# A two-layer graph network with residual norms: attention in float32 blocks, once a group, beside layer 0

## The chip, the cores and the metric

The kernel runs on one core of a Trainium2 chip. The metric is the device time of one execution in microseconds: 678.2 as the median of 3 runs (678.11 to 678.23). The core has five engines that run side by side, each with its own queue: TensorE (PE, its weight loads as PEld), VectorE (DVE), ScalarE (ACT), GpSimd (POOL) and SyncE (SP), which here issues the DMAs.

## What is computed

x is (128, 64, 512) in float32: 128 graphs of 64 nodes with 512 features. adj is 64 x 64 and shared. `reference`, cut to what matters:

```python
x = layernorm(x + einsum('bnf,nm->bmf', x, adj * adj) + bias)            # layer 0; its result is h
z_l, z_g, v = h @ W_lang.T, h @ W_grav.T, h @ W_V.T
A_l = relu(cos(z_l, z_l)) * not_eye                                       # 64 x 64 a graph
A_g = exp(-dist2(z_g, z_g) / (2 sigma^2)) * not_eye
K = w_l * rownorm(A_l * adj) + (1 - w_l) * rownorm(A_g * adj)
out = layernorm(h + (K @ v) @ W_O.T)                                      # layer 1
```

## The kernel before

It works on 16 groups (g) of 8 graphs. A group is held as 4 tiles (p) of 128 rows x 512, each tile two graphs of 64 nodes. The weights are folded once in a setup: T_L = W_lang'W_lang and T_G likewise (as the blocks of a triangle), and M = W_V'W_O'. So a group needs 12 projections (`project`, L360): 4 blocks each of y_L = T_L h and y_G = T_G h, and 4 tiles of u = h M. The float32 values are written as a sum of two float32r numbers, hi and lo, and a product is three float32r matmuls (hi·hi, hi·lo, lo·hi, from `parts`). So a projection of 128 x 512 has 3, 6, 9 or 12 matmuls of 512 columns: 108 in a group. They go through a ring of three PSUM banks: ACT rounds a bank to hi (`hi_proj`), DVE subtracts hi from it to get lo (`lo_proj`), and then the bank is free.

Attention takes a half group (q) at a time, two pairs of graphs. `gram` (L380) multiplies h by y for a pair (128 rows), both similarities in one matmul of 256 columns, 24 matmuls a half; since a pair's 128 x 128 result covers both graphs, its off-diagonal 64 x 64 blocks mean nothing and are zeroed by the mask `adj_bd`. ACT copies the result to P (`copy_p`), DVE takes its diagonal (`diagonals`) and subtracts it (shift), POOL makes inverse norms (`columns`), PE transposes P and the norms (`transpose_p`, L393 and L400), DVE adds, weighs and normalises (`similarities`, `coefficients`, `combine`), PE transposes K (`transpose_k`, L411), ACT and DVE split it, and `apply_k` (L424) multiplies K' by u with 3 matmuls of 512 columns for each p. POOL also makes the scale and the bias of both layernorms from DVE's counts; ACT applies them.

`layer0` (L320) is different: it is plain float32, and its 4 matmuls are blocks of 64 x 64 that lie in the four quarters of the array (`tile_position`), reading two 64-row halves of x and writing two halves of two banks:

```python
last = pe.matmul((bank_x, bank_p)[a][cols, :], mix[rows, rows], x_sb[g % 2][rows, 2 * h + c, :],
                 start=True, stop=True, tile_position=(a * N, c * N))
```

The order of work is written by hand, for each engine in a function `step(g)`: the projections of g, between them the second half of the attention of g - 1, layer 0 and the transposes of h of g + 1, and the gram of g. Semaphores hold the engines together. The last group and the end have an order of their own. DVE, ACT and POOL run their steps in a loop (`Fori`); PE's program is written out.

Of the kernel before, what the change touches and what calls it, by code (L numbers as in the profile page):

```python
# [5 lines left out]
def bass_two_layer_graph_resnorm(  # L19
# [13 lines left out]
    fp32r = mybir.dt.float32r  # L33
    ALU = mybir.AluOpType
    ACT = mybir.ActivationFunctionType

    B, N, D = x.shape
    R = 128
# [10 lines left out]
    PROJ = [(L, 3), (L, 0), (L, 2), (L, 1), (G, 3), (G, 0), (G, 2), (G, 1)] + [("u", p) for p in range(NP)]  # L49
# [4 lines left out]
    assert NG % 2 == 0 and NPROJ % NRING == 0  # L54

    def ring_of(k):

        return (NSETUP + k) % NRING

# [5 lines left out]
    with ctx:  # L65
# [8 lines left out]


        ident = sb("ident", [R, R])
        off_diag = sb("off_diag", [R, R])
        adj_bd = sb("adj_bd", [R, R])
        mask = sb("mask", [R, R])
        mix = sb("mix", [R, R])  # L80
# [5 lines left out]
        mixw = sb("mixw", [R, 4])  # L86
        pow_neg_half = sb("pow_neg_half", [R, 2])
# [7 lines left out]
        h_sb = [sb(f"h_sb{i}", [R, NP, D]) for i in range(2)]  # L95
# [9 lines left out]
        P_sb = [sb(f"P_sb{q}", [R, 2, 2, R]) for q in range(2)]  # L105
        diag_scr = sb("diag_scr", [R, 4, R])
        S2 = sb("S2", [R, 2, 2, R])
        X0 = sb("X0", [R, 2, R])
        X_l = sb("X_l", [R, 2, R])
        E_g = sb("E_g", [R, 2, R])  # L110
        X_g = sb("X_g", [R, 2, R])
        K_l = sb("K_l", [R, 2, R])
        K_sb = sb("K_sb", [R, 2, R])
        KT_hi = [sb(f"KT_hi{q}", [R, 2, R], fp32r) for q in range(2)]
        KT_lo = [sb(f"KT_lo{q}", [R, 2, R], fp32r) for q in range(2)]

        sq = [sb(f"sq{q}", [R, 2, 2]) for q in range(2)]
        sq_floor = [sb(f"sq_floor{q}", [R, 2]) for q in range(2)]
        inv_norm = [sb(f"inv_norm{q}", [R, 2]) for q in range(2)]
        sq_eps = [sb(f"sq_eps{q}", [R, 2]) for q in range(2)]  # L120
        floors = [sb(f"floors{q}", [R, 4]) for q in range(2)]
        sums = sb("sums", [R, 4])
        dens = sb("dens", [R, 4])
        recs = sb("recs", [R, 4])
        coef = sb("coef", [R, 4])
# [13 lines left out]
        o_sb = sb("o_sb", [R, NP, D])  # L139


        w_raw = [sb("w_raw", [R, DC, D]), o_sb, h_sb[1]]
        yT_w = [t[:, :, :, :].rearrange("p a s t -> p (a s t)") for t in (yT_hi, yT_lo)]

        def half(view, k):
            return view[:, k * DC * D:(k + 1) * DC * D].rearrange("p (c d) -> p c d", c=DC)

        W_hi = [half(yT_w[0], 0), half(yT_w[0], 1), u_hi[:, :, :], hT_hi[1][:, :, :]]
        W_lo = [half(yT_w[1], 0), half(yT_w[1], 1), u_lo[:, :, :], hT_lo[1][:, :, :]]

# [31 lines left out]
        x0_loaded = [sem(f"x0_loaded{c}") for c in range(2)]  # L182
# [51 lines left out]

        block = ctx.enter_context(nc.Block())

        def p_bank(g, q):

            return last_p_ps if isinstance(g, int) and g == NG - 1 and q else p_ps

        def out_rows(g):

            return x_sb[0] if isinstance(g, int) and g == NG - 1 else o_sb

        def kt_bank(g):

            return last_kt_ps if isinstance(g, int) and g == NG - 1 else kt_ps
# [893 lines left out]
```

## Time and profile before

| | |
|---|---|
| median of 3 runs | 678.2 us (678.11 to 678.23) |
| the profiled execution | 680.26 us, of which its span is 678.1 |
| PE, PEld busy | 663.6 us (98%), 542.8 us (80%) |
| DVE, ACT, POOL busy | 503.2 us (74%), 314.8 us (46%), 134.4 us (20%) |
| mean granted TensorE clock | 0.991 of full |
| one step in the middle | 39.17 us |

A span goes from the first to the last instruction; the execution's time has 2.16 us around it. Matmuls are pipelined: a row's duration holds its way through the array, and what a matmul costs in a row of them is the distance from its start to the next start. A step is the stretch from the first matmul of `project(g, 0)` to that of `project(g + 1, 0)`.

### The profile page before, as it was taken

To read this page: it belongs to the slowest core of one execution; us is meant where nothing else is said; L and a number is where in the kernel's file an instruction comes from. 1 tells how busy PE (TensorE), PEld (TensorE's weight loads), DVE (VectorE), ACT (ScalarE), POOL (GpSimd) and SP (SyncE) were. 2 spreads that over 40 slices of the span, in tenths; PEclk is the share of its full clock that TensorE was granted. 3 is DMA by queue.
4 is the path that set the end of the run, shared out by engine and by line. 5 is a ranking of instruction groups with operands and counts; after the bars stand their busy time and mean duration, and the time that the engine had idled before them with its cause. 6 is when DMAs were issued, how large, how long until landed. Compare 5 with 4: busy or idle time off the path is not lost.

```text
span 678.1 us, 11268 instructions
## 1 busy us (share of the span) xinstructions
PE 663.6 (98%) x3643; PEld 542.8 (80%) x3643; DVE 503.2 (74%) x1517; ACT 314.8 (46%) x580; POOL 134.4 (20%) x394
## 2 busy tenths in 40 slices
PE   7999999999999999999999999999999999999994
PEld 5887978878797887879787887878788787978883
DVE  2845496877959686895968688696868869596886
ACT  2733445444454545444454544444454454445433
POOL 0200202131221213122121313112121311302122
PEclk8999999999999999999999999999999999999998
DMA  8701104021030403003030401303040120001002
GB/s 256 196 1 24 38 1 126 1 91 34 33 94 21 104 1 108 16 35 91 31 94 1 122 4 49 76 32 94 0 125 1 65 59 32 32 1 63 0 32 93
DMA packets 20695, 38.61 MB, mean 57 GB/s; under 512 B 2096, under 2 KB 2096, under 8 KB 20656
## 3 DMA queue, kind: packets, MB, share of 16 engines
q1 hardware_dynamic: 20656, 38.05, 19.7%
q8 instruction: 29, 0.48, 0.3%
q14 instruction: 10, 0.08, 0.0%
HBM read 21.27 MB, written 16.78 MB: 56 GB/s over the span
## 4 chain that ended last, share of the span: by engine, by line
PE 96%; DVE 1%; DMA 1%; ACT 1%; SPq 0%; issue 0%; POOL 0%; POOLq 0%; DVEq 0%
PE ring L360 59%; PE bank_p L380 13%; PE bank_x L320 5%; PE ring L476 4%; PE bank_k L424 3%; PE bank_r L424 3%; PE bank_pt L393 2%; PE bank_r L400 1%; PE bank_pt L339 1%; PE bank_r L339 1%; PE bank_k L339 1%; DMA w_raw<-in_L_gnn_W_lang_dram 1%; PE bank_pt L411 1%; PE bank_x L339 1%; PE bank_x L380 0%; DVE z_bn L844 0%
## 5 line engine op out<-in xcount | busy, mean ns | idle before, releaser
L360 PE MATMUL ring<-hT_hi,T_hi 128*128 128x512 f32 x320 | 129.3, 404 | 0.0
L562 ACT ACTIVATE yT_hi<-ring 128x512 fp32r<-128x512 f32 x128 | 75.9, 593 | 112.0 <-PE ring L360 111.9
L360 PE MATMUL ring<-hT_hi,T_lo 128*128 128x512 f32 x320 | 125.4, 392 | 0.0
L360 PE MATMUL ring<-hT_lo,T_hi 128*128 128x512 f32 x320 | 124.8, 390 | 0.0
L757 DVE TENSOR_TENSOR yT_lo<-ring,yT_hi 128x512 fp32r<-128x512 f32 x128 | 87.5, 683 | 31.5 <-ACT yT_hi L562 31.5
L360 PE MATMUL ring<-M_hi,hT_hi 128*128 128x512 f32 x256 | 105.3, 411 | 0.0
L360 PE MATMUL ring<-M_hi,hT_lo 128*128 128x512 f32 x256 | 100.5, 392 | 0.0
L360 PE MATMUL ring<-M_lo,hT_hi 128*128 128x512 f32 x256 | 99.6, 389 | 0.0
L601 ACT ACTIVATE o_sb<-o_sb,z_nb,z_rs 128x512 f32<-128x512 f32 x60 | 47.1, 809 | 61.6 <-POOL z_nb L1054 61.6
L360 PEld LDWEIGHTS ring<-M_hi,hT_hi 128*128 128x128 f32 x256 | 48.0, 188 | 32.6 <-issue 13.0
L380 PE MATMUL bank_p<-yT_hi,hT_hi 128*128 128x256 f32 x248 | 71.4, 288 | 0.0
L360 PEld LDWEIGHTS ring<-hT_hi,T_lo 128*128 128x128 f32 x320 | 60.1, 188 | 13.5
L380 PE MATMUL bank_p<-yT_hi,hT_lo 128*128 128x256 f32 x248 | 70.1, 283 | 0.0
L380 PE MATMUL bank_p<-yT_lo,hT_hi 128*128 128x256 f32 x248 | 70.1, 283 | 0.0
L360 PEld LDWEIGHTS ring<-hT_lo,T_hi 128*128 128x128 f32 x320 | 60.4, 189 | 10.7
L360 PEld LDWEIGHTS ring<-hT_hi,T_hi 128*128 128x128 f32 x320 | 60.2, 188 | 10.6
L757 DVE TENSOR_TENSOR u_lo<-ring,u_hi 128x512 fp32r<-128x512 f32 x64 | 44.2, 691 | 24.1 <-ACT u_hi L562 24.0
L566 ACT ACTIVATE h_sb<-h_sb,y_nb,y_rs 128x512 f32<-128x512 f32 x64 | 48.6, 807 | 25.0 <-POOL y_nb L1054 25.0
L1049 POOL TENSOR_SCALAR z_ve<-z_mv 128x2 f32<-128x2 f32 x32 | 7.0, 218 | 264.2 <-DVE z_mv L853 259.5
L752 DVE TENSOR_TENSOR hT_lo<-bank_x,hT_hi 128x512 fp32r<-128x512 f32 x16 | 11.0, 690 | 62.0 <-ACT hT_hi L562 62.0
L360 PEld LDWEIGHTS ring<-M_hi,hT_lo 128*128 128x128 f32 x256 | 48.0, 188 | 11.0
L360 PEld LDWEIGHTS ring<-M_lo,hT_hi 128*128 128x128 f32 x256 | 48.2, 188 | 8.8
(146 smaller groups left out, 1301.7 us busy)
## 6 DMA issues: line engine op xcount, KB each, us to landing
x_sb<-in_x_dram SPq DMA_DIRECT2D x30, 512.0 KB, 6.4
out_dram<-o_sb SPq DMA_DIRECT2D x60, 256.0 KB, 2.0
x_sb<-in_x_dram SPq DMA_DIRECT2D x4, 256.0 KB, 5.5
w_raw<-in_L_gnn_W_lang_dram SPq DMA_DIRECT2D x1, 1024.0 KB, 6.6
o_sb<-in_L_gnn_W_grav_dram SPq DMA_DIRECT2D x1, 1024.0 KB, 9.3
h_sb<-in_L_gnn_W_V_dram SPq DMA_DIRECT2D x1, 1024.0 KB, 11.3
w_raw<-in_L_gnn_W_O_dram SPq DMA_DIRECT2D x1, 1024.0 KB, 10.0
out_dram<-x_sb SPq DMA_DIRECT2D x4, 256.0 KB, 2.0
```

Of the source, the lines that this page charges most:

```text
L320: last = pe.matmul((bank_x, bank_p)[a][cols, :], mix[rows, rows], x_sb[g % 2][rows, 2 * h + c, :], start=True, stop=True, tile_position=(a ...
L339: last = pe.transpose(hT_banks[p][:, s], h_sb[par][:, p, s], ident[:, :])
L360: last = pe.matmul(bank[:, :], a, b, start=n == 0, stop=n == len(terms) - 1)
L380: last = pe.matmul(p_bank(g, q)[:, pp, :, :], a, b, start=n == 0, stop=n == len(terms) - 1)
L393: last = pe.transpose(pt_ps[:, pp, s, :], P_sb[q][:, pp, s, :], ident[:, :])
L424: last = pe.matmul(bank[:, :], a[:, p % 2, :], b[:, p, :], start=n == 0, stop=n == 2)
L476: last = pe.matmul(ring[at % NRING][:, 0:cols], a, b, start=n == 0, stop=n == len(terms) - 1)
L562: return act.activation(dst, src, ACT.Copy, scale=scale)
L566: act.activation(h_sb[par][:, p, :], h_sb[par][:, p, :], ACT.Identity, scale=y_rs[:, p:p + 1], bias=y_nb[:, p:p + 1]).then_inc(h_ready, 1)
L601: act.activation(out_rows(g)[:, p, :], out_rows(g)[:, p, :], ACT.Identity, scale=z_rs[:, p:p + 1], bias=z_nb[:, p:p + 1]).then_inc(o_ready, 1)
L752: dve.tensor_tensor(hT_lo[par][:, :, s], hT_banks[p][:, :].rearrange("p (c r) -> p c r", c=DC), hT_hi[par][:, :, s], ALU.subtract).then_in ...
L757: dve.tensor_tensor(proj_dst(k, 1), ring[ring_of(k)][:, :], proj_dst(k, 0), ALU.subtract).then_inc(proj_split, 1)
```

## The change

- Gram and `apply_k` no longer work on split numbers. y, u, K' and a copy of h' (`hT`) are kept in plain float32. ACT alone empties the ring (`evict`), and `lo_proj`, `lo_kt`, `hi_kt` are gone. h' is still split for the projections, so ACT now copies each tile of h' twice (`hi_hT`, `copy_hT`) and `lo_hT` reads both from SBUF.
- The zero blocks are gone. Only the 64 x 64 blocks of a graph with itself are computed and held, so four pairs fit into where two were: one P, S, K for a group. Gram is 32 matmuls of 64 rows of result and 128 columns, two side by side in the left and the right half of the array. All of attention's steps between gram and K' happen once a group; the diagonals and row sums are a multiplication and a reduction instead of a fused operation, and `scale_l` moves from ACT into a multiplication on DVE (`combine`).
- `apply_k` is 4 float32 matmuls for two p, in the quarters of the array as in layer 0, and stands right behind layer 0. It writes to banks of its own.
- The outputs are made in place in h (three buffers) instead of in `o_sb`. All loops are written out. W_O is loaded without a wait, and in the setup W_V comes after it.

The diff at its core (what has the same form elsewhere is left out):

```diff
-        yT_hi = sb("yT_hi", [R, DC, 2, GT], fp32r)
-        yT_lo = sb("yT_lo", [R, DC, 2, GT], fp32r)
-        u_hi = sb("u_hi", [R, NP, D], fp32r)
-        u_lo = sb("u_lo", [R, NP, D], fp32r)
...
+        hT = [sb(f"hT{i}", [R, DC, GT]) for i in range(2)]
+        yT = sb("yT", [R, DC, 2, GT])
+        u_sb = sb("u_sb", [R, NP, D])
...
+        bank_y = [pb(f"bank_y{a}") for a in range(2)]
+        bank_z = [pb(f"bank_z{a}") for a in range(2)]
+        bank_s = pb("bank_s")
...
-                        last = pe.matmul((bank_x, bank_p)[a][cols, :], mix[rows, rows], x_sb[g % 2][rows, 2 * h + c, :],
+                        last = pe.matmul(bank_y[a][half(c), :], mix[half(a), :], x_sb[g % 2][half(a), 2 * h + c, :],
...
+            def gram(g):
+                pe.wait_ge(proj_out, NPROJ * g + 2 * DC)
+                pe.wait_ge(hT_copied, NP * g + NP)
+                if g > 0:
+                    pe.wait_ge(kt_copied, g)
+                for h in range(2):
+                    for a in range(2):
+                        for i in range(DC):
+                            for c in range(2):
+                                t = slice((4 * h + 2 * c + a) * N, (4 * h + 2 * c + a + 1) * N)
+                                last = pe.matmul(p_ps[half(c), h, :, a, :], hT[g % 2][:, i, t], yT[:, i, :, t],
+                                                 start=i == 0, stop=i == DC - 1, tile_position=(0, c * N))
+                last.then_inc(gram_done, 1)
...
-                    terms = [(a[:, i, s], b[:, i, :, s]) for i in range(DC)
-                             for a, b in parts(hT_hi[par], hT_lo[par], yT_hi, yT_lo)]
-                    for n, (a, b) in enumerate(terms):
-                        last = pe.matmul(p_bank(g, q)[:, pp, :, :], a, b, start=n == 0, stop=n == len(terms) - 1)
...
+            def apply_k(g, h):
+                pe.wait_ge(kt_copied, g + 1)
+                pe.wait_ge(proj_out, NPROJ * g + 2 * DC + 2 * h + 2)
+                if h:
+                    pe.wait_ge(z_added, NP * g + 2)
+                elif g < NG - 1:
+                    pe.wait_ge(hT_split, NP * g + 2 * NP)
+                    pe.wait_ge(hT_copied, NP * g + 2 * NP)
                 else:
+                    pe.wait_ge(z_added, NP * g)
+                for c in range(2):
+                    for a in range(2):
+                        last = pe.matmul(bank_z[a][half(c), :], KT[half(a), h, half(c)], u_sb[half(a), 2 * h + c, :],
+                                         start=True, stop=True, tile_position=(a * N, c * N))
+                last.then_inc(ku_done, 2)
-                for n, (a, b) in enumerate(parts(KT_hi[p // 2], KT_lo[p // 2], u_hi, u_lo)):
-                    last = pe.matmul(bank[:, :], a[:, p % 2, :], b[:, p, :], start=n == 0, stop=n == 2)
...
+            def step(g, tail=True):
+                project(g, 0)
+                project(g, 1)
+                project(g, 2)
+                if tail:
+                    transpose_k(g - 1)
+                layer0(g + 1, 0)
                 if tail:
                     apply_k(g - 1, 0)
+                project(g, 3)
+                project(g, 4)
+                project(g, 5)
+                layer0(g + 1, 1)
+                if tail:
                     apply_k(g - 1, 1)
+                project(g, 6)
+                transpose_h(g + 1, 0)
+                project(g, 7)
+                project(g, 8)
+                gram(g)
+                transpose_h(g + 1, 1)
+                project(g, 9)
+                transpose_h(g + 1, 2)
+                transpose_p(g)
+                transpose_h(g + 1, 3)
+                project(g, 10)
+                project(g, 11)
+                rows(g)
...
+            def evict(g, k):
+                kind, j = PROJ[k]
                 act.wait_ge(proj_done, NPROJ * g + k + 1)
+                dst = u_sb[:, j, :] if kind == "u" else yT[:, j, kind, :]
+                copy(dst, ring[ring_of(k)][:, :]).then_inc(proj_out, 1)
...
-            def hi_proj(g, k):
-                copy(proj_dst(k, 0), ring[ring_of(k)][:, :]).then_inc(proj_hi, 1)
...
-            def lo_proj(g, k):
-                dve.wait_ge(proj_hi, NPROJ * g + k + 1)
-                dve.tensor_tensor(proj_dst(k, 1), ring[ring_of(k)][:, :], proj_dst(k, 0),
-                                  ALU.subtract).then_inc(proj_split, 1)
...
+            def lo_hT(g, p):
                 dve.wait_ge(hT_hi_done, NP * g + p + 1)
+                dve.wait_ge(hT_copied, NP * g + p + 1)
+                dve.tensor_tensor(hT_view(hT_lo[g % 2], p), hT_view(hT[g % 2], p), hT_view(hT_hi[g % 2], p),
+                                  ALU.subtract).then_inc(hT_split, 1)
...
+            for g in range(1, NG - 1):
+                step(g)
```

The first place is PE in the first third of a step, around layer 0 (`bank_x`, `bank_p` before, `bank_y` now). Before, on PE:

```order
L411 MATMUL bank_pt<-ident,K_sb 128x128 x2
L320 MATMUL bank_x<-x_sb,mix 64x512
L320 MATMUL bank_p<-x_sb,mix 64x512
L320 MATMUL bank_x<-x_sb,mix 64x512
L320 MATMUL bank_p<-x_sb,mix 64x512
...
L424 MATMUL bank_k<-u_hi,KT_hi 128x512
L424 MATMUL bank_k<-u_lo,KT_hi 128x512
L424 MATMUL bank_k<-u_hi,KT_lo 128x512
L424 MATMUL bank_r<-u_hi,KT_hi 128x512
L424 MATMUL bank_r<-u_lo,KT_hi 128x512
L424 MATMUL bank_r<-u_hi,KT_lo 128x512
```

Now, on PE (L294 is layer 0, L387 `apply_k`):

```order
L330 MATMUL ring<-hT_hi,T_lo 128x512
L370 MATMUL bank_s<-ident,K_sb 128x128 x2
L294 MATMUL bank_y<-x_sb,mix 64x512 x4
L387 MATMUL bank_z<-u_sb,KT 64x512 x4
L330 MATMUL ring<-hT_hi,T_hi 128x512
```

The same stands a second time in a step, behind `project(g, 5)`, without the transposes. The 6 full matmuls for two p have become 4 block matmuls behind layer 0's.

The second place is PE around gram. Before (24 matmuls in each of two halves, the second behind `project(g, 11)`):

```order
L360 MATMUL ring<-M_hi,hT_lo 128x512
L380 MATMUL bank_p<-yT_hi,hT_hi 128x256
L380 MATMUL bank_p<-yT_lo,hT_hi 128x256
L380 MATMUL bank_p<-yT_hi,hT_lo 128x256
...
L380 MATMUL bank_p<-yT_hi,hT_lo 128x256
L339 MATMUL bank_x<-ident,h_sb 128x128 x4
L339 MATMUL bank_k<-ident,h_sb 128x128 x4
```

Now (L344 is gram, L353 P's transposes, L363 those of the norms, at the step's end behind `project(g, 11)`):

```order
L330 MATMUL ring<-M_hi,hT_lo 128x512
L344 MATMUL bank_s<-yT,hT 64x2x64 x32
L309 MATMUL bank_y<-ident,h_sb 128x128 x4
...
L309 MATMUL bank_z<-ident,h_sb 128x128 x4
L353 MATMUL bank_s<-ident,P_sb 128x128 x4
L309 MATMUL bank_z<-ident,h_sb 128x128 x4
...
L363 MATMUL bank_y<-ident,inv_rep 128x128 x2
```

Gram stands once, behind `project(g, 8)`, and the transposes of P and of the norms are in the same step behind it, where they were in the next step, twice.

The third place is DVE from the end of gram to K (S2 is shown as S, and X0 and X as X):

```order
L681 TENSOR_TENSOR diag_scr<-P_sb,ident_c 128x512
L686 TENSOR_REDUCE sq<-diag_scr 128x8
L676 TENSOR_TENSOR hT_lo<-hT,hT_hi 128x4x2x64
L693 TENSOR_TENSOR P_sb<-P_sb,sq 128x2x128
L765 BN_AGGR z_mv<-z_bn 128x2 x2
L676 TENSOR_TENSOR hT_lo<-hT,hT_hi 128x4x2x64
L701 TENSOR_TENSOR S<-bank_s,P_sb 64x4x64 x4
L676 TENSOR_TENSOR hT_lo<-hT,hT_hi 128x4x2x64 x2
L710 SCALAR_TENSOR_TENSOR X<-S,bank_y 64x2x64 x4
...
L739 TENSOR_TENSOR XW<-X,coef 128x512
L747 TENSOR_TENSOR K_sb<-XW 128x256
```

All of it stands in one row in step g, with the four `lo_hT` between; before, it was spread over the first half of step g + 1 between the 12 `lo_proj`.

## Rows read from the trace of the kernel before

**Rows 1.** The page's part 1 (engines) and part 4 (chain by engine)

```profile
PE 663.6 (98%) x3643; PEld 542.8 (80%) x3643; DVE 503.2 (74%) x1517; ACT 314.8 (46%) x580; POOL 134.4 (20%) x394
...
PE 96%; DVE 1%; DMA 1%; ACT 1%; SPq 0%; issue 0%; POOL 0%; POOLq 0%; DVEq 0%
```

**Rows 2.** Windows, step 7: stretch, us, busy PE, PEld, DVE, ACT, POOL, clock, DMA, GB/s

```profile
315.26:354.43 39.17, 39.17 (x218) 31.91 (x217) 30.23 (x93) 18.68 (x34) 8.23 (x25) 1.00 0.19 54
```

**Rows 3.** Timeline of PE: start of steps 0, 1 and 15 (start us, us)

```profile
45.74 0.39 PE L360 MATMUL ring<-hT_hi,T_hi 128*128 128x512 f32 x1
...
80.26 0.40 PE L360 MATMUL ring<-hT_hi,T_hi 128*128 128x512 f32 x1
...
628.60 0.40 PE L360 MATMUL ring<-hT_hi,T_hi 128*128 128x512 f32 x1
```

**Rows 4.** Timeline of PE in step 7: apply_k, K's transposes, layer 0

```profile
329.19 0.39 PE L424 MATMUL bank_k<-u_hi,KT_hi 128*128 128x512 f32 x1
...
330.55 0.39 PE L360 MATMUL ring<-hT_hi,T_hi 128*128 128x512 f32 x1
...
331.92 0.38 PE L411 MATMUL bank_pt<-ident,K_sb 128*128 128x128 f32 x2
332.23 0.64 PE L320 MATMUL bank_x<-x_sb,mix 64*64 64x512 f32 x1
...
332.71 0.59 PE L320 MATMUL bank_x<-x_sb,mix 64*64 64x512 f32 x1
...
333.25 0.50 PE L360 MATMUL ring<-M_hi,hT_hi 128*128 128x512 f32 x1
333.58 0.40 PE L360 MATMUL ring<-M_lo,hT_hi 128*128 128x512 f32 x1
```

**Rows 5.** Timeline of PE in step 7: gram's half, then 8 transposes of h

```profile
344.18 0.28 PE L380 MATMUL bank_p<-yT_hi,hT_hi 128*128 128x256 f32 x1
...
346.94 0.28 PE L380 MATMUL bank_p<-yT_hi,hT_lo 128*128 128x256 f32 x1
347.06 0.60 PE L339 MATMUL bank_x<-ident,h_sb 128*128 128x128 f32 x4
347.49 0.60 PE L339 MATMUL bank_k<-ident,h_sb 128*128 128x128 f32 x4
347.85 0.47 PE L360 MATMUL ring<-M_hi,hT_hi 128*128 128x512 f32 x1
348.16 0.39 PE L360 MATMUL ring<-M_lo,hT_hi 128*128 128x512 f32 x1
```

**Rows 6.** Groups by line: layer 0 into one of its two banks

```profile
L320 PE MATMUL bank_x<-x_sb,mix 64*64 64x512 f32 x128 | 34.6, 614 | 0.0
```

**Rows 7.** Timeline of PEld in layer 0 of step 7

```profile
332.28 0.13 PEld L320 LDWEIGHTS bank_x<-x_sb,mix 64*64 64x64 f32 x1
```

**Rows 8.** Timeline of PE in the setup: 128 columns a matmul

```profile
20.89 0.27 PE L476 MATMUL ring<-yT_lo,yT_hi 128*128 128x128 f32 x1
21.00 0.28 PE L476 MATMUL ring<-yT_hi,yT_lo 128*128 128x128 f32 x1
```

**Rows 9.** Timelines of ACT and DVE in step 8, behind the second gram

```profile
354.63 0.60 ACT L562 ACTIVATE P_sb<-bank_p 128x512 f32<-128x512 f32 x1 [2.17 <-PE bank_p L380]
...
355.39 0.29 DVE L767 CUSTOM_DVE_ANT_0 diag_scr<-P_sb,ident 128x128 f32<-128x128 f32 x1 [0.55 <-ACT P_sb L562]
```

**Rows 10.** Groups by line: DVE and POOL

```profile
L788 DVE TENSOR_TENSOR S<-bank_pt,P_sb 128x512 f32<-128x512 f32 x32 | 21.8, 680 | 0.6 <-PE bank_pt L393 0.6
L795 DVE SCALAR_TENSOR_TENSOR X<-S,bank_r 128x256 f32<-128x256 f32 x32 | 13.5, 421 | 3.3
L1051 POOL TENSOR_TENSOR y_rs<-y_ve,pow_neg_half 128x2 f32<-128x2 f32 x32 | 22.9, 717 | 2.7
```

**Rows 11.** Chain in order of time: the end

```profile
663.55 0.68 PE bank_r L424 x3
...
674.09 0.81 ACT x_sb L601
```

More of the change, by code:

```diff
@@ L659, in hi_row, with hi_value @@
                 last.then_inc(setup_hi, 1)
+            def hi_value(dst, at):
+                for i in range(DC):
+                    act.wait_ge(setup_done, at + i + 1)
+                    copy(dst[:, i, :], ring[(at + i) % NRING][:, :]).then_inc(setup_hi, 1)
             hi_weight(0)
@@ L675, in _ @@
                 if i >= 2:
-                    normalise_h(0, 0, i)
-            def hi_value(dst, at):
-                for i in range(DC):
-                    act.wait_ge(setup_done, at + i + 1)
-                    copy(dst[:, i, :], ring[(at + i) % NRING][:, :]).then_inc(setup_hi, 1)
+                    normalise_h(0, i)
             hi_value(W_hi[3], 2 * DC)
             for p in range(NP):
-                hi_hT(0, 0, p)
+                copy_hT(0, p)
+                hi_hT(0, p)
             hi_value(M_hi, 3 * DC)
-            step(0, 0, tail=False)
@@ L707, in _ @@
-            hi_kt(g - 1, 1)
-            hi_proj(g, 7)
-            copy_p(g, 0)
+            step(0, tail=False)
+            for g in range(1, NG - 1):
+                step(g)
+            g = NG - 1
+            evict(g, 0)
+            copy_kt(g - 1)
+            evict(g, 1)
+            evict(g, 2)
+            evict(g, 3)
+            evict(g, 4)
+            evict(g, 5)
+            evict(g, 6)
+            evict(g, 7)
+            copy_p(g)
             normalise_out(g - 1, 0)
-            copy_p(g, 1)
+            evict(g, 8)
@@ new lines, in shift, with add_p @@
+            def shift(g):
+                dve.wait_ge(sq_done, g + 1)
+                settle(dve)
+                dve.tensor_tensor(P_sb[:, :, G, :, :], P_sb[:, :, G, :, :],
+                                  sq[:, :, G, :].unsqueeze(3).broadcast_to([R, 2, 2, N]),
+                                  ALU.subtract).then_inc(shift_done, 1)
+            def add_p(g):
+                dve.wait_ge(pt_done, g + 1)
+                for c in range(2):
+                    for a in range(2):
+                        last = dve.tensor_tensor(S2[half(c), :, :, a, :], pt_ps[half(a), :, :, half(c)],
+                                                 P_sb[half(c), :, :, a, :], ALU.add)
+                last.then_inc(s2_done, 1)
@@ L913, in _ @@
+                shift(g)
+                if tail:
+                    gather_z(g - 1, 1)
+                lo_hT(g + 1, 1)
+                add_p(g)
+                lo_hT(g + 1, 2)
+                lo_hT(g + 1, 3)
+                weigh(g)
+                coefficients(g)
+                combine(g)
             dve.wait_ge(ident_ready, 2)
-            dve.tensor_scalar(off_diag[:, :], ident[:, :], -1.0, 1.0, ALU.mult, ALU.add).then_inc(mix_steps, 1)
+            dve.tensor_tensor(ident_c[:, :], ident[:, 0:N], ident[:, N:R], ALU.add).then_inc(mix_steps, 1)
@@ L1015, in _ @@
[L1015 to L1029 removed]
+            step(0, tail=False)
+            for g in range(1, NG - 1):
+                step(g)
@@ new lines, in _ @@
+            g = NG - 1
+            add_z(g - 1, 0)
+            add_z(g - 1, 1)
+            diagonals(g)
+            shift(g)
+            count_z(g - 1, 0)
+            count_z(g - 1, 1)
+            gather_z(g - 1, 0)
+            add_z(g - 1, 2)
+            add_p(g)
+            weigh(g)
+            coefficients(g)
+            combine(g)
+            add_z(g - 1, 3)
+            count_z(g - 1, 2)
+            count_z(g - 1, 3)
+            gather_z(g - 1, 1)
+            add_z(g, 0)
+            add_z(g, 1)
@@ L1088, in _ @@
+                columns(g)
             pool.memset(ident[:, :], 0.0).then_inc(ident_ready, 1)
```

888 lines of the change are left out of this document (346 added, 542 removed).

## The prediction

> **What bounds the kernel now.** I read the page's busy shares and its chain first: PE is busy 98% of the span, the chain runs over PE for 96% of it, DVE is at 74% and ACT at 46% [rows 1]. Then one step by windows: of 39.17 us PE is busy for all 39.17, at the full clock, with DVE at 30.2 [rows 2]. The fourteen steps from 1 to 14 take (628.60 - 80.26) / 14 = 39.17 each [rows 3], so one step speaks for all. PE never waits there. What DVE and ACT are spared is thus worth nothing by itself (12 `lo_proj` a step, 0.68 us each [rows 10], all beside PE); what counts is what PE issues, and whether the new waits stay behind it.
>
> **PE's step, priced.** The distance between starts is the price. A projection's matmul: (331.92 - 330.55) / 6 = 0.228 us [rows 4], so 108 cost 24.7. Gram: (347.06 - 344.18) / 24 = 0.12 [rows 5], 48 cost 5.76. `apply_k`: 330.55 - 329.19 = 1.36 for two p [rows 4], 2.72 a step. Layer 0: 1.02 from its first start to the next operation, 0.1 to get in (332.23 - 331.92 less two transposes) and 0.1 lost by the first matmul behind it (0.33 where 0.228 is usual) [rows 4]: 1.22, twice. Transposes: 8 in 0.79, about 0.1 each, and 0.08 for the matmul behind them (0.31 where 0.228 is usual) [rows 5]; 32 of them with five such joints are 3.6. The sum is 24.7 + 5.76 + 2.72 + 2.44 + 3.6 = 39.2, as measured.
>
> **The change, part by part.** The projections stay: 24.7. Layer 0 stays: 2.44.
>
> `apply_k` becomes four float32 blocks behind layer 0. Layer 0 is the same shape, so it gives the price. The program has 64 such matmuls into `bank_x`, the trace 128 [rows 6]: each is recorded as two. The eight records of one layer 0 start at 332.23 and at 332.71 and are over at 333.25 [rows 4]; so four run at a time, 0.48 a slot. Two slots are 0.96, and the way in and out is paid by layer 0 already. I take 1.0, twice 2.0: it saves 0.72. Bounds: 0.96, and 1.22 if it paid its own way.
>
> Transposes: 24 instead of 32 (8 fewer for P, norms and K), with three joints: 2.4 + 0.25 = 2.65, saving 0.95.
>
> Gram is the term that no row shows: 32 float32 matmuls, so 64 records, of 128 columns, two side by side over all 128 rows. By the stream, a slot of layer 0 has 512 columns and 0.48 us, so 128 columns are 0.12. By the weights, a 128-wide load each leaves 0.11 between starts [rows 8], and two 64-wide loads are as wide. So a slot of two records costs 0.11 to 0.13; I take 0.125, 32 slots are 4.0, and 0.3 for changing the array's division in and out, as layer 0 pays 0.2 and there are more blocks here: 4.3, saving 1.45. The low end is 32 x 0.111 = 3.55. The high end is that no two records overlap: 64 x 0.12 = 7.7, and 0.3. I take the low half because the weights of layer 0's second slot are loaded at 332.28 [rows 7], while the first slot runs to 332.71, and because its blocks share rows in pairs, too.
>
> The new step: 24.7 + 2.44 + 2.0 + 2.65 + 4.3 = 36.1, which is 3.07 less.
>
> **Do the new waits stay hidden?** DVE's durations follow 0.16 us + 0.001 a column (680 ns at 512, 421 at 256 [rows 10]), so 0.29 at 128. Three joints:
> - Gram to the transposes of P. 0.2 until ACT copies, 0.76 to DVE's start [rows 9], the multiplication 0.72 with its semaphore, the reduction 0.6, one `lo_hT` 0.6 in between, the shift 0.46: 3.35. PE has four transposes, `project(g, 9)` of 2.8 and four more: 3.65. Slack 0.3.
> - Norms to K's transposes. DVE adds up to 0.4 (PE to DVE), four narrow `weigh` 0.9, then it waits for `exp_g`, which stands behind `evict(g, 11)` and a `normalise_out` on ACT and is over at 1.95 (0.2 to start, 0.5 for the first, 0.7 for a scaling that lasts 0.81 [rows 11], an estimated 0.55 for 256 columns); then 0.46, reduction 0.72, three small ones 0.6, product 0.8, sum 0.5: 5.1. PE has `project(g + 1, 0)` to `(2)`, 24 matmuls, 5.5, and the norms' own 0.3. Slack 0.65.
> - h' to `project(g + 1, 0)`: `copy_hT(g + 1, 3)` stands behind `evict(g, 10)` on ACT, then `lo_hT`: 2.1 behind `project(g, 10)`, where PE has 2.7 and 0.3 more. Slack 0.9.
> POOL's norms begin behind the shift, `gather_z` and a `scale_z` of 1.6, and take about 2.2 (a power is 717 ns [rows 10]): ready 2.5 before PE asks. POOL's copy `inv_rep` has no row; it may take 0.2 or 2 us and stays hidden. ACT's second copy of h' (4 x 0.6) fits into the idle half of ACT. Since the joints are thin, I add 0.1 a step.
>
> **The sum.** Step 0 (34.52 now [rows 3]) has no attention of a group before it, but now holds the transposes of P and norms: 24.7 + 2.44 + 2.2 + 0.25 + 4.3 = 33.9, -0.6. Steps 1 to 14: 14 x -3.07 = -43.0. Step 15 to the end is 678.10 - 628.60 = 49.5 [rows 3]. New: PE until its last projection 24.7 + 0.3 + 2.4 + 4.3 + 0.8 = 32.5; K's transposes and copy 0.9; `apply_k` 1.1; two additions 1.3, since the banks must be free; `apply_k` 1.3 until DVE starts; five DVE operations and their small ones 3.7; POOL 2.0; and 4.0 from the last scaling on, as now (674.09 to 678.10 [rows 11]; PE's last multiplication stood at 663.55 there). That is 46.8, -2.7. The setup: the first matmuls wait for W_lang as before; the eight copies of h' on ACT lie beside M's 10.9 us of matmuls: 0. Loops written out: no row shows a wait for instructions with PE's program written out already: 0. Total -46.3, and +1.6 for the joints: -44.7. The profiled execution of 680.26 would be 635.6; the median stands 2.1 below that execution, so I predict 633.5.
>
> **A rule against it.** Before, every load of weights lies behind the matmul in front of it although both use all rows: 0.12 a matmul in gram, of which 0.11 are the load alone [rows 5, 8]. The Trainium skill (TensorE: Matmul & The Clock Gate, Part 3) says that a load overlaps a matmul in flight only when their row groups differ (its Part 2 names a background weight buffer as a second way), and the new gram has all its tiles in the same row groups. The trace of before disagrees with that as it stands. If it held for gram's two halves, the 64 loads would be laid bare; that case is the second rival.
>
> **The rivals.**
> - *Gram's halves take turns* (slower). Over all 128 rows the two column halves do not stream at once. 64 x 0.12 + 0.3 = 8.0, 3.7 more a step: 633.5 + 59 = 692. It speaks for it that only quarters were seen side by side; against it, that two quarters on the same 64 rows read different data in one slot. The change turns slower once gram costs over 4.3 + 44.7 / 16 = 7.1. Chance 0.07.
> - *Gram's weight loads are bare.* Half of 0.11 for each of 64 records is 3.5 more a step: 689. Chance 0.03.
> - *A joint gives way.* An operation of DVE or ACT with these broadcast or cut-up operands takes longer than its width says, and PE waits 1 us a step at P's or K's transposes: 633.5 + 16 = 649. The slacks of 0.3 and 0.65 speak for it. Chance 0.16.
> - *`apply_k` runs two blocks at a time*, twice the slots: +1.9 a step, 664. Against it: layer 0's rows. Chance 0.03.
> - *Gram at its low end and no joint late*: -0.85 a step, 620. Chance 0.12.
>
> **The numbers.** Forecast 0.59, for 624 to 644. The range that leaves out the last cases reaches from 620 to 658. A measurement tells 0.2% from no change, 1.4 us; only a gram between the rivals gives that: 0.02. Slower: 0.10; faster: 0.88.
>
> **What would show it.** Right: a step of 36 us with PE without a gap, gram's starts 0.12 to 0.13 a pair, `apply_k` 1.0 behind layer 0, 64 records of gram a step. Wrong: gaps of PE before P's transposes released by DVE's shift, or before K's by DVE's sum (joints); gram at 8 us (turns, bare loads); DVE above ACT in waits of the projections would mean that the ring is held by something I left out.

## The result, and the profile after

| | before | after |
|---|---|---|
| median of the runs, us | 678.22 (678.11 to 678.36, 4 runs) | 619.66 (618.78 to 620.79, 4 runs) |
| the profiled execution, its time and its span, us | 680.26, 678.1 | 618.78, 617.0 |
| ratio after / before | | 0.9137, 95% interval [0.912, 0.9155] |
| a step, us | 39.17 | 35.30 |

58.6 us faster by the medians, where 44.7 were predicted. The sign was right, and so was what bounds the kernel; the forecast of 633.5 was 13.8 too high. The result lies 4.3 below the range of the forecast (624 to 644) and 0.3 below the low end of the wider one (620). One price in the sum was wrong, that of a slot (a slot is two or four records that run side by side).

The page of the changed kernel, parts 1 and 4 (beside [rows 1]), and the window of its step 7 with the columns of [rows 2]:

```profile
PE 599.9 (97%) x3835; PEld 462.2 (75%) x3835; DVE 355.9 (58%) x798; ACT 301.3 (49%) x532; POOL 131.5 (21%) x344
...
PE 93%; DMA 2%; DVE 1%; SPq 1%; ACT 1%; issue 0%; POOL 0%; POOLq 0%
```

```profile
289.51:324.81 35.30, 35.30 (x232) 27.04 (x230) 21.07 (x47) 17.88 (x31) 8.18 (x21) 1.00 0.22 60
```

PE is still busy for the whole step at the full clock. DVE lost 9.2 us a step and ACT 0.8; the step lost 3.87. Where PE's time went stands in its timeline (start us, us), step 7 of the changed kernel, with the projections' matmuls in between left out:

```profile
302.25 1.09 PE L294 MATMUL bank_y<-x_sb,mix 64*64 64x512 f32 x8
303.16 1.04 PE L387 MATMUL bank_z<-u_sb,KT 64*64 64x512 f32 x8
304.13 0.50 PE L330 MATMUL ring<-hT_hi,T_hi 128*128 128x512 f32 x1
304.47 0.40 PE L330 MATMUL ring<-hT_lo,T_hi 128*128 128x512 f32 x1
...
310.65 0.39 PE L330 MATMUL ring<-M_hi,hT_lo 128*128 128x512 f32 x1
310.97 3.71 PE L344 MATMUL bank_s<-yT,hT 128*64 128x128 f32 x64
314.61 0.66 PE L309 MATMUL bank_y<-ident,h_sb 128*128 128x128 f32 x4
315.02 0.48 PE L330 MATMUL ring<-M_hi,hT_hi 128*128 128x512 f32 x1
...
317.87 0.60 PE L309 MATMUL bank_z<-ident,h_sb 128*128 128x128 f32 x4
318.31 0.60 PE L353 MATMUL bank_s<-ident,P_sb 128*128 128x128 f32 x4
318.74 0.60 PE L309 MATMUL bank_z<-ident,h_sb 128*128 128x128 f32 x4
319.10 0.47 PE L330 MATMUL ring<-M_hi,hT_hi 128*128 128x512 f32 x1
```

Read by distances between starts, as in the prediction:
- **Gram** (L344): 64 records from 310.97 to the next operation at 314.61, 3.64 us. The matmul ahead would be over at 310.65 + 0.228 = 310.88, so the way in is 0.09. Together 3.73 against 5.76 before [rows 5]: 2.03 saved.
- **Layer 0 and `apply_k`** (L294, L387): 0.91 and 0.97, with 0.08 in and 0.11 out (0.34 instead of 0.228 at 304.13): 2.07. Layer 0 by itself cost 1.22 before [rows 4], so `apply_k` adds 0.85, twice 1.70, against 2.72: 1.02 saved.
- **Transposes**: K's 0.23, h' 0.44 and 0.50, h', P, h' 1.32, norms' 0.23, each with what the matmul behind loses: 2.72 against 3.6: 0.88 saved.

24.7 + 3.73 + 4.14 + 2.72 = 35.3, the step as measured, and 2.03 + 1.02 + 0.88 = 3.9 are the 3.87 saved. Only the saving by fewer transposes has no experiment of its own below.

Inside these groups the slots are not alike. A narrow window shows the start of a later slot, once the records before it are over. The second and the fourth slot of layer 0 and `apply_k`, and then the second and the last pair of gram:

```profile
302.73 0.61 PE L294 MATMUL bank_y<-x_sb,mix 64*64 64x512 f32 x4
303.59 0.61 PE L387 MATMUL bank_z<-u_sb,KT 64*64 64x512 f32 x4
311.13 0.39 PE L344 MATMUL bank_s<-yT,hT 128*64 128x128 f32 x4
314.40 0.28 PE L344 MATMUL bank_s<-yT,hT 128*64 128x128 f32 x2
```

Layer 0 and `apply_k` are four slots that start at 302.25, 302.73, 303.16 and 303.59 and are over at 304.13: 0.48, 0.43, 0.43 and 0.54. Gram's first slot takes 0.16 (310.97 to 311.13), the 30 behind it (314.40 - 311.13) / 30 = 0.109 each, and the last 0.21 (to 314.61). So a slot inside a stream costs 0.43 for 512 columns and 0.109 for 128; the first slot behind another cut of the array costs 0.05 more and the last 0.10 to 0.11 more.

There is no gap at a joint. The wait list of PE in the whole execution holds nothing that comes back each step. Its three longest (us in total, times, longest):

```profile
PE ring L431 <- DVE W_own L816: 2.9, 1, 2.9
PE bank_s L437 <- POOL ident L959: 1.5, 1, 1.5
PE bank_z L387 <- DVE h_sb L751: 1.5, 1, 1.5
```

### The profile page after: what moved, and what is told of

It is laid out like the page before. It is cut to its first block, busy times and chain, and to the rows that moved or that the text cites. A ratio compares the mean times of both kernels' runs of the same rounds, so it can differ in the third digit from the quotient of the medians.

```text
span 617.0 us, 10089 instructions
## 1 busy us (share of the span) xinstructions
PE 599.9 (97%) x3835; PEld 462.2 (75%) x3835; DVE 355.9 (58%) x798; ACT 301.3 (49%) x532; POOL 131.5 (21%) x344
## 4 chain that ended last, share of the span: by engine, by line
PE 93%; DMA 2%; DVE 1%; SPq 1%; ACT 1%; issue 0%; POOL 0%; POOLq 0%
PE ring L330 65%; PE bank_s L344 9%; PE bank_y L294 5%; PE bank_z L387 5%; PE bank_y L309 3%; DMA h_sb<-in_L_gnn_W_V_dram 2%; PE bank_z L309 2%; PE ring L431 2%; PE bank_s L353 1%; PE bank_s L370 1%; PE bank_y L363 1%; SPq L236 0%; DVE hT_lo L816 0%; ACT hT_hi L492 0%; DVE h_sb L751 0%
## 5 line engine op out<-in xcount | busy, mean ns | idle before, releaser
L492 ACT ACTIVATE yT<-ring 128x512 f32<-128x512 f32 x128 | 76.4, 598 | 99.4 <-PE ring L330 98.1
L660 DVE TENSOR_TENSOR h_sb<-bank_y,bias_bc 128x512 f32<-128x512 f32 x64 | 42.4, 686 | 68.6 <-PE bank_y L294 68.5
L492 ACT ACTIVATE u_sb<-ring 128x512 f32<-128x512 f32 x64 | 38.0, 597 | 82.7 <-PE ring L330 82.7
L537 ACT ACTIVATE h_sb<-h_sb,z_nb,z_rs 128x512 f32<-128x512 f32 x63 | 49.3, 807 | 27.3 <-POOL z_nb L923 27.3
L676 DVE TENSOR_TENSOR hT_lo<-hT,hT_hi 128x512 fp32r<-128x512 f32 x64 | 45.0, 703 | 29.4 <-ACT hT_hi L492 16.3
L681 DVE TENSOR_TENSOR diag_scr<-P_sb,ident_c 128x512 f32<-128x512 f32 x16 | 11.1, 692 | 86.9 <-ACT P_sb L492 86.9
L344 PEld LDWEIGHTS bank_s<-yT,hT 128*64 128x64 f32 x1024 | 55.6, 137 | 6.1 <-issue 5.3
L918 POOL TENSOR_SCALAR y_ve<-y_mv 128x2 f32<-128x2 f32 x32 | 7.6, 237 | 243.7 <-DVE y_mv L670 243.7
L344 PE MATMUL bank_s<-yT,hT 128*64 128x128 f32 x1024 | 59.4, 274 | 0.0
L751 DVE TENSOR_TENSOR h_sb<-bank_z,h_sb 128x512 f32<-128x512 f32 x64 | 43.2, 677 | 13.0 <-PE bank_z L387 12.9
```

What stands on the lines that cost most here:

```text
L344: last = pe.matmul(p_ps[half(c), h, :, a, :], hT[g % 2][:, i, t], yT[:, i, :, t], start=i == 0, stop=i == DC - 1, tile_position=(0, c * N))
L492: return act.activation(dst, src, ACT.Copy, scale=scale)
L537: act.activation(h_sb[g % 3][:, p, :], h_sb[g % 3][:, p, :], ACT.Identity, scale=z_rs[:, p:p + 1], bias=z_nb[:, p:p + 1]).then_inc(o_ready, 1)
L660: dve.tensor_tensor(h_sb[g % 3][:, p, :], bank_y[p % 2][:, :], bias_bc[:, :], ALU.add).then_inc(y_added, 1)
L676: dve.tensor_tensor(hT_view(hT_lo[g % 2], p), hT_view(hT[g % 2], p), hT_view(hT_hi[g % 2], p), ALU.subtract).then_inc(hT_split, 1)
L681: dve.tensor_tensor(diag_scr[:, :, :], P_sb[:, :, :, :, :].rearrange("r h s a j -> r (h s a) j"), ident_c[:, :].unsqueeze(1).broadcast_to( ...
```

## The experiments

All edits are made to the changed kernel. Times are medians, steps are distances between two norms' transposes in the middle of the execution.

**1. Why does gram take 3.64 us?** Four kernels: the halves in runs of four matmuls, one half alone, whole blocks, and the halves entirely apart. Two of them are for their time only: e2 leaves half of P stale, and e3 puts its results elsewhere and takes the exponential of 0.

```diff
-for a in range(2):
-    for i in range(DC):
-        for c in range(2):
+for a in range(2):
+    for c in range(2):
+        for i in range(DC):
```

> Same gram, but the four matmuls of one column half come in a row, then the four of the other. Theory (the two halves stream at once, because neighbours in the program lie in different halves): a pair of records took 0.114 us in the changed kernel; in a row each record takes that 0.114 by itself, 64 x 0.114 = 7.3 for one gram in place of 3.65, with some overlap where the half changes. Step 35.3 to about 38.6 to 38.9, 16 x 3.3 to 3.6 us more: 672 to 678 us. Rival (a 64-wide tile costs 0.057 by itself, whatever stands beside it): gram stays at 3.65 and the time at 619.7.

```diff
-for c in range(2):
+for c in range(2 if g == 0 else 1):
```

> The second column half of every gram is left out from step 1 on, so half of P is stale; 32 records of gram instead of 64. Theory (halves at once): what is left takes as long as the pair did, 32 x 0.114 = 3.65 us; step 35.3, time 619.7 or 1 less. Rival (0.057 a record by itself): gram 1.85 us, 15 x 1.8 = 27 less, 593 us.

```diff
-for h in range(2):
-    for a in range(2):
-        for i in range(DC):
-            for c in range(2):
...
+for p in range(NP):
+    for i in range(DC):
+        t = slice(p * R, (p + 1) * R)
+        last = pe.matmul(p_ps[:, p % 2, :, :, :].rearrange("r s a j -> r s (a j)"),
+                         hT[g % 2][:, i, t], yT[:, i, :, t],
+                         start=i == 0, stop=i == DC - 1)
```

> Gram in float32 but in whole 128 x 128 blocks as before the change (16 matmuls of 256 columns, 32 records), so the zero blocks are computed again; its results lie in other places of the bank, and the exponential is taken of 0 so that all stays finite. Theory (a float32 record streams at the same pace as layer 0's, 0.91 / 2 = 0.455 for 512 columns): 0.23 a record, 7.3 for a gram, 3.65 more a step: 16 x 3.65 = 58 more, 678 us, no better than the kernel before. Rival (the record of 256 columns takes 0.12 as the old gram's matmuls did): 3.8, 620 us, and leaving out the zero blocks brought nothing.

After these three came the fourth, with c as the outermost loop:

```diff
+for c in range(2):
     for h in range(2):
         for a in range(2):
             for i in range(DC):
-                for c in range(2):
```

> All 32 records of gram's first column half come before all 32 of the second. With the halves alternating by one matmul gram took 3.64 us, by runs of four (8 records) 4.47, and one half by itself 3.64 for 32 records, 0.114 each. Theory (a half's records each take 0.114, the other half runs beside them only as far as it stands within a few records in the program): 64 x 0.114 = 7.3 less some 0.4 at the one seam, 6.9; step 3.25 more, 16 x 3.25 = 52, 672 us. Rival (PE looks over a whole gram, so order does not matter beyond the 0.8 of e1): 4.5 to 5, 634 to 640 us.

Gram's row and the start of the operation behind it, timelines of PE of e1, e2, e3 and e10 in this order:

```profile
317.18 4.54 PE L344 MATMUL bank_s<-yT,hT 128*64 128x128 f32 x64
321.65 0.65 PE L309 MATMUL bank_y<-ident,h_sb 128*128 128x128 f32 x4
```

```profile
312.03 3.71 PE L344 MATMUL bank_s<-yT,hT 128*64 128x128 f32 x32
315.67 0.66 PE L309 MATMUL bank_y<-ident,h_sb 128*128 128x128 f32 x4
```

```profile
296.51 7.07 PE L342 MATMUL bank_s<-yT,hT 128*128 128x256 f32 x32
303.42 0.60 PE L309 MATMUL bank_y<-ident,h_sb 128*128 128x128 f32 x4
```

```profile
294.70 6.82 PE L344 MATMUL bank_s<-yT,hT 128*64 128x128 f32 x64
301.45 0.66 PE L309 MATMUL bank_y<-ident,h_sb 128*128 128x128 f32 x4
```

| order of gram | records | gram, us | time, us |
|---|---|---|---|
| halves alternate (the change) | 64 | 3.64 | 619.66 |
| one half alone (e2) | 32 | 3.64 | 619.61 |
| runs of four matmuls (e1) | 64 | 4.47 | 633.8 |
| one half, then the other (e10) | 64 | 6.75 | 671.1 |
| whole blocks, zeros too (e3) | 32 of 256 columns | 6.91 | 669.94 |

Four things follow. Leaving a half out saves nothing (e2: the same 3.64 us), so the second half runs wholly beside the first. With the halves apart nearly the whole doubling comes back (e10), and the time is that of whole blocks with their zeros (e3). Without them side by side, float32 would have been no gain for gram: e3's 6.91 is above the 5.76 of the three fp32r products, and of the 58.6 us e3 gives back 50.3. And in e1 both my numbers were wrong: neither 7.3 nor 3.65.

How far apart two halves may stand is in the traces of e10 and e1. The records of gram in 1 us of e10, inside its first half and around the seam (stretch, us, busy PE with the records that run in it, clock, DMA, GB/s), and then in 1 us of the changed kernel:

```profile
296.00:297.00 1.00, 1.00 (x12) 1.00 0.11 29
297.70:298.70 1.00, 1.00 (x15) 1.00 0.11 33
```

```profile
312.00:313.00 1.00, 1.00 (x24) 1.00 0.00 0
```

Taken record by record, the starts around the seam are 297.80, 297.81, 297.91, 297.97, 298.02, 298.08, 298.13 and 298.19, where elsewhere one starts every 0.109 us. The records don't name their half, but these are two trains with that distance: the last four records of the first half (its 29th to 32nd) and the first four of the second, whose first start lies 0.006 behind the 29th's. e1 has the same at each of its seven seams, always at the fifth of a run's eight records. So a run of one half begins four records, that is two matmuls, before the other's has ended. Four slots of 0.109 less the 0.05 of a first slot are 0.385 saved at a seam: with one seam 64 x 0.109 + 0.15 - 0.385 = 6.74 (6.75 measured), with seven 4.43 (4.47). Why it is four, no run shows.

**2. What does `apply_k` pay by itself?**

```diff
                 if tail:
                     transpose_k(g - 1)
                 layer0(g + 1, 0)
+                project(g, 3)
                 if tail:
                     apply_k(g - 1, 0)
-                project(g, 3)
```

> The first apply_k of a step stands behind project(g, 3) and no longer right behind layer 0, so it pays its own way in and out. Theory of the prediction (0.2 us for both): 14 x 0.2 = 2.8 more, 622.4 us. From the trace of the changed kernel: 0.08 in and 0.11 out, also 0.19. Rival (nothing is paid between differently cut matmuls, or the later addition of z holds up the banks): 619.7, or above 625 with a gap of PE in front of transposes of h.

625.57 us, 5.9 more; the step is 35.69, 0.39 more, without a gap:

```profile
300.87 1.09 PE L294 MATMUL bank_y<-x_sb,mix 64*64 64x512 f32 x8
301.89 0.50 PE L330 MATMUL ring<-hT_hi,T_hi 128*128 128x512 f32 x1
302.23 0.40 PE L330 MATMUL ring<-hT_lo,T_hi 128*128 128x512 f32 x1
...
303.17 0.39 PE L330 MATMUL ring<-hT_hi,T_lo 128*128 128x512 f32 x1
303.49 1.09 PE L387 MATMUL bank_z<-u_sb,KT 64*64 64x512 f32 x8
304.51 0.50 PE L330 MATMUL ring<-hT_hi,T_hi 128*128 128x512 f32 x1
```

By itself it costs what layer 0 costs: 1.02, 0.09 in and 0.11 out, 1.22. Behind layer 0 it costs 0.85. So being neighbours saves 0.37, not the 0.2 of entry and exit alone: apart, each of the two has a first slot of 0.48 and a last of 0.54; together there is one of each, and the two slots between take 0.43. What a place costs is 0.09 in, 0.05 in its first slot, 0.11 in its last and 0.11 in the matmul behind, 0.36. The expectation had half of it, 0.2.

**3. How thin are the joints?** Two spare DVE multiplications of 512 columns, in front of the shift (e5) or of K's product (e6); the semaphores of the spare operations are left out here and in experiment 4.

```diff
+                for i in range(2):
+                    dve.tensor_tensor(spare[i][:, :, :], bias_bc[:, :].rearrange("r (k j) -> r k j", k=8),
+                                      ident_c[:, :].unsqueeze(1).broadcast_to([R, 8, N]), ALU.mult)
```

> Two spare DVE multiplications of 512 columns in front of the shift, some 1.2 to 1.3 us later. In the changed kernel the shift ended at 317.71 and the transposes of P began at 318.31, 0.6 later. Theory (that joint is as thin as this): PE waits some 0.65 to 0.75 there, 15 or 16 times, 10 to 12 more: 630 to 632 us. By the 0.3 of the prediction it would be 0.95 a step, 635. Rival (the room is larger than the trace lets one see, DVE idles 5.4 us before): 619.7.

> The same two spare multiplications in front of the product that makes K. In the changed kernel the sum for K ended at 329.78 and K's transposes began at 330.37, 0.55 later. Theory: PE waits 0.65 to 0.75 a step there, 10 to 11 more: 630 us; by the 0.65 of the prediction 0.6 a step, 629. Rival: no wait, 619.7.

e5: 631.99 us, step 36.07. e6: 627.93 us, step 35.83. The timeline of DVE in e5:

```profile
323.78 1.29 DVE L696 TENSOR_TENSOR spare<-bias_bc,ident_c 128x512 f32<-128x512 f32 x2
324.98 0.42 DVE L701 TENSOR_TENSOR P_sb<-P_sb,sq 128x256 f32<-128x256 f32 x1
```

and of PE:

```profile
324.36 0.60 PE L311 MATMUL bank_z<-ident,h_sb 128*128 128x128 f32 x4
325.55 0.63 PE L355 MATMUL bank_s<-ident,P_sb 128*128 128x128 f32 x4 [0.58 <-DVE P_sb L701]
```

The same two for e6:

```profile
334.97 0.42 DVE L755 TENSOR_TENSOR K_sb<-XW 128x256 f32<-128x256 f32 x1
```

```profile
334.73 0.39 PE L332 MATMUL ring<-hT_hi,T_lo 128*128 128x512 f32 x1
335.45 0.44 PE L372 MATMUL bank_s<-ident,K_sb 128*128 128x128 f32 x2 [0.33 <-DVE K_sb L755]
```

In e5 the shift moved by 1.20 and P's transposes start 1.19 behind the four in front of them, where 0.44 is usual: 0.75 late. The slack was 1.20 - 0.75 = 0.45. In e6 K's sum moved by 1.0 only (a semaphore's way became hidden behind the spare work), and the transposes start 0.49 late: slack 0.5. The "idle" in brackets is less than the delay in both, because it counts from the modelled end of a pipelined matmul. The joints are about as thin as predicted (0.3 and 0.65) and hold; each tenth beyond them would be paid 15 times. The expectation of e6 was too high: it had a wait of 0.65 to 0.75, or 0.6 by the prediction, and 0.5 came.

**4. Is what DVE was spared worth anything?** Five spare operations where DVE idles 5.4 us in front of P's diagonals.

```diff
+                for i in range(5):
+                    dve.tensor_tensor(spare[i][:, :], bias_bc[:, :], bias_bc[:, :], ALU.mult)
                 diagonals(g)
```

> Five spare DVE operations of 512 columns a step (3 to 3.4 us, 0.16 x 5 more in issue at most) where DVE idles 5.4 us in front of P's diagonals. Theory (what DVE is spared is worth nothing, since PE sets the step): 619.7 us and the same 35.30 a step. Rival (DVE's relief brought part of the gain): 15 x 3 = 45 more, 665 us.

620.02 us, and the step is 35.30 as before, with this in each step of DVE:

```profile
309.76 3.08 DVE L794 TENSOR_TENSOR spare<-bias_bc 128x512 f32<-128x512 f32 x5
315.24 0.69 DVE L683 TENSOR_TENSOR diag_scr<-P_sb,ident_c 128x512 f32<-128x512 f32 x1 [2.40 <-ACT P_sb L494]
```

3.1 us of DVE a step cost nothing in this place, and 1.2 us cost 0.5 to 0.8 a step in front of a joint. It is the place that counts. Only DVE was loaded; that ACT's relief is worth nothing too rests on PE having no gap.

**5. Can transposes and cut-up matmuls be put together?**

```diff
-                transpose_h(g + 1, 0)
                 project(g, 7)
                 project(g, 8)
                 gram(g)
+                transpose_h(g + 1, 0)
```

> The first transposes of h' move from between project(g, 6) and (7) to the end of gram, beside the second ones; the copies and the low part move with them. Theory (a group of transposes costs 0.09 for the matmul behind it, and gram's exit is paid once): 0.1 less a step, 15 x 0.1 = 1.5 less, 618.2 us. Rival (ACT, which now has five copies in a row behind gram, is late for project(g, 9) or the ring): slower, above 621.

619.53 us, step 35.27: no difference in the time, 0.03 in the step. Eight transposes in a row take 0.43 more than four, and four by themselves cost 0.35 and 0.09 for the matmul behind them, 0.44. A separate group of transposes costs nothing extra; my term of 0.08 a joint is only the last transpose's own end.

```diff
-                layer0(g + 1, 1)
-                if tail:
-                    apply_k(g - 1, 1)
                 project(g, 6)
-                transpose_h(g + 1, 0)
                 project(g, 7)
                 project(g, 8)
+                layer0(g + 1, 1)
+                if tail:
+                    apply_k(g - 1, 1)
                 gram(g)
+                transpose_h(g + 1, 0)
```

> Layer 0's second half and the second apply_k move from behind project(g, 5) to right in front of gram, and the first transposes of h' to right behind it; DVE's and ACT's order follows. Theory (going from whole matmuls to cut-up ones and back costs 0.09 in and 0.11 out, and the drain in front of it: e4's split cost 0.39 a step): one way in and out is saved, 0.2 to 0.4 less a step, 15 x = 3 to 6 less: 614 to 617 us. Rival (the second half's h' is ready later and DVE's chain to P and K has only some 0.6 to 0.8 of room): gaps of PE at P's or h's transposes, 620 to 635 us.

615.73 us (615.45 to 617.66, 5 runs), ratio to the kernel before 0.9069 [0.9049, 0.9089]; step 35.04, 0.26 less. It beats both kernels: 3.9 us or 0.6% under the change, which is the step's 0.26 x 15, and the intervals of the two ratios lie apart. The timeline of PE in its step 7:

```profile
307.49 0.39 PE L330 MATMUL ring<-M_hi,hT_lo 128*128 128x512 f32 x1
307.81 1.09 PE L294 MATMUL bank_y<-x_sb,mix 64*64 64x512 f32 x8
308.72 1.04 PE L387 MATMUL bank_z<-u_sb,KT 64*64 64x512 f32 x8
309.68 3.71 PE L344 MATMUL bank_s<-yT,hT 128*64 128x128 f32 x64
313.33 1.09 PE L309 MATMUL bank_y<-ident,h_sb 128*128 128x128 f32 x8
```

Gram follows `apply_k` at once, 0.96 behind its start, so gram's way in (0.09) and the exit of 0.11 are gone; e7's 0.03 is in the 0.26 too. Record by record, `apply_k`'s last slot still takes 0.54 and gram's first still 0.16: between quarters and halves of the array the ends of the slots are paid as before. So bringing differently cut work together saves some 0.2, work of the same cut 0.37.

**6. The setup.** W_lang loaded first, and in e12 also two rows of G's product taken before W_V, on top of e11.

```diff
+            load_w(0, w_lang)
             load_x(0, x0_loaded[0], slice(0, 2))
             for c in range(2):
                 sp.dma_start(adj_c[half(c), :], adj).then_inc(adj_loaded, 16)
-            load_w(0, w_lang)
```

> The load of W_lang is issued first, in front of x and adj. Theory (the setup is bound by W_lang: landing, four copies, four low parts, then the first product at 10.50 after a wait of 2.85): W_lang lands some 1 us sooner, the first product at 9.5, 1 less: 618.7 us. Rival (x and adj then land later than the 27 warm-up transposes end and layer 0 holds up PE, or a later load sets the setup's end): 619.7 or more.

> The same and the setup: W_lang's load first, and ACT takes the first two rows of G's product before W_V, for whose load it otherwise waits. Theory: 1.2 less by the first (the profiled span of e8 was 615.8 against 617.0), 0 to 0.8 by the second: e11 less 1 to 2 us. Rival: the setup is bound by the last load, no difference from e11.

e8: 619.16 us (617.55 to 620.0), where 618.7 was expected and the change has 619.66. e12: 616.62 us (615.56 to 617.24), where e11 had 615.73. No gain is shown. PE's layer 0 and its first product, in the change and then in e8:

```profile
6.56 1.09 PE L294 MATMUL bank_y<-x_sb,mix 64*64 64x512 f32 x8
10.50 1.87 PE L431 MATMUL ring<-W_own 128*128 128x512 f32 x7 [2.85 <-DVE W_own L816]
```

```profile
9.40 1.09 PE L294 MATMUL bank_y<-x_sb,mix 64*64 64x512 f32 x8 [1.87 <-DVE mix L809]
10.41 1.89 PE L431 MATMUL ring<-W_own 128*128 128x512 f32 x7
```

What the rival of e8 names first is in its trace. W_lang did land sooner (ACT starts on it at 6.19, not at 9.09), but `adj`, now behind it, landed later (DVE begins `mix` at 8.86, not at 5.85), so layer 0 held up PE and the first product came only 0.09 sooner. e12 has the same wait, 3.3 us. Step 0 began at 42.38 in e8's profile, at 44.44 in the change's and at 46.85 in e12's. In the eleven profiles with the setup as the change has it, it began anywhere from 44.33 (e13) to 47.62 (e4). In e4 PE waited 5.4 us for W_lang's product, where it waits 2.9 in the change: W_lang was 8.0 us from issue to landing in e4 and 5.6 in the change. A microsecond of the setup can't be read from one profile of each kernel.

## Why the prediction was wrong, and what of it was right

- **The step that failed** is the price of a slot: "so four run at a time, 0.48 a slot". It was read from layer 0's first slot, which holds 0.05 of entry; inside a stream a slot of 512 columns takes 0.43. Layer 0's second slot, 0.54, was in the same rows and holds the exit. The price went into both new terms, `apply_k` (two slots, 0.96) and gram (a quarter of it, 0.12, rounded up to 0.125), and the ends that the 0.48 and 0.54 hold were not seen as ends.
- **PE bounds it, and what DVE and ACT are spared is worth nothing.** Right: 39.17 and 35.30 are PE's own sums, and for DVE e13 shows it on the chip.
- **Gram, 4.3.** Right in kind, 0.57 too high: the largest miss, 16 x 0.57 = 9 us. The 0.125 for a slot of two records measured 0.109, and 32 of them make 0.5 of the 0.57. The weights' row had pointed there: 0.11 [rows 8]. The 0.3 "for changing the array's division in and out" was nearly right: 0.09 in, 0.05 in the first slot and 0.10 in the last are 0.24. But it was raised from layer 0's 0.2 "as there are more blocks", and that reason is wrong: these ends are paid once per place. The rivals *take turns* and *bare loads* are excluded by e2. The weights' row stands beside it, PEld in step 7 of the changed kernel: 64 loads in 3.47 us, inside gram's 3.64.

```profile
310.96 3.47 PEld L344 LDWEIGHTS bank_s<-yT,hT 128*64 128x64 f32 x64 [0.35 <-issue]
```

- **The rule against it.** In e2 32 loads filled the same 3.47 us as the 64 of the change, though all lie in the same row groups: the added loads are hidden behind matmuls in flight. And a slot takes 0.109 for 128 columns, 0.216 for 256 (e3: 6.91 / 32) and 0.43 for 512: it follows the columns, with nothing left over for the loads. The Trainium skill (TensorE: Matmul & The Clock Gate, Part 3) lets a load overlap a matmul in flight only for differing row groups; the measurement decides against that sentence as it stands, as the trace of before already did. The background weight buffer that the prediction names from the same page would allow it; no run here can show that buffer. The same page's section Why this matters for your kernels says that small column tiles run concurrently as small row tiles do; the runs agree (3.64 us for one half and for two), as long as the halves stand next to each other.
- **`apply_k`, 1.0 each, with 0.96 as the low bound.** It measured 0.85, below the bound. It is the wrong slot again: two slots inside the stream are 2 x 0.43 = 0.86. That layer 0 already pays the way in and out was right (e4: 1.22 by itself). 2 x 0.15 = 0.3 a step, 14 x 0.3 = 4 us.
- **Transposes, 2.65.** 2.72 measured. Right, though e7 shows that their joints are no price of their own.
- **The joints.** Slacks of 0.3, 0.65 and 0.9 were predicted; measured were 0.45 (e5) and 0.5 (e6). For h' there are only the rows, 324.81 - 324.03 = 0.78; the same reading gives 0.6 at the two others, 0.1 more than the experiments. None ran out, so the allowance of 0.1 a step, 1.6 us, was not needed, and *a joint gives way* did not come true. DVE's operations with broadcast operands took what their width says: 0.69 for the multiplication (0.72 with its semaphore was assumed).
- **The sum.** Steps 1 to 14: 14 x 3.87 = 54.1 instead of 43.0. Step 0: 77.71 - 44.44 = 33.27, 1.25 less instead of 0.6. Step 15 to the end: 617.0 - 571.91 = 45.1, 4.4 less instead of 2.7; of the 1.7 more, 0.8 lie in PE's part (most of it gram) and 0.8 in DVE's and POOL's behind the last `apply_k`. Together 59.8 of the 61.1 by which the two spans differ. The other 1.3 are the setup, which was put at 0 and whose own spread is larger. The medians differ by 58.6, since the profiled execution of before stood 2.0 above its median and that of after 0.9 below.
- **The chances.** The case *gram at its low end and no joint late*, -0.85 a step, gave 620, and 619.66 came. That is in part luck: gram did not reach its low end (3.73, not 3.55), and `apply_k`, which the case left at 1.0, brought the rest. It got 0.12 because I read each unknown from the middle of its bounds; the two terms with the wrong slot and the allowance for the joints, all off to the same side, made some 14 us.

## What to carry to other kernels

Cutting a matmul's zero blocks away saves nothing by itself: the two halves one after the other took as long as the whole blocks (e10, e3). The gain is in the order, with the tiles of different parts of the array alternating in the program, and then in putting all cut-up work in one place, since each place costs 0.36 us to enter and leave (less is saved, some 0.2, where the cuts differ). When PE bounds a kernel, price each stage by distances between starts, and the inside of a stream apart from its first and last slot, and for the engines beside it look at the slack in front of each joint, not at their share.

## What the runs showed of the hardware

- Two matmuls on different column halves of the array overlap even when they don't alternate, but only within four records, two float32 matmuls (e1, e10). I had expected all or nothing.
- In a stream, a float32 record takes 0.109 us for 128 columns in a half tile (e2), 0.216 for 256 over the whole array (e3: 6.91 / 32) and 0.43 for 512 in a quarter. The time goes by the columns streamed, not by the size of the tile, and half or quarter tiles side by side share it.
- Changing how the array is cut costs PE 0.36 us a place: 0.09 in front, 0.05 in the first slot, 0.11 in the last, 0.11 in the whole matmul behind (e4).
- With one and the same setup, the start of step 0 differed by up to 3.3 us between profiled executions (e13, e4). In e4 W_lang alone took 2.4 us longer to land than in the change.
